# Score matmuls of two steps in one visit, one output chunk and one small product behind them, three score banks, and no loops, in an attention kernel on one core

## The chip, the cores and the metric

The kernel runs on one core of one Trainium2 chip. Its time is the device time of one execution in microseconds (us). PE is the matrix engine (TensorE), DVE is VectorE, ACT is ScalarE, POOL is GpSimd; SP is SyncE, which issues all transfers.

## The reference

Two layers on x of 8 batches x 512 positions x 128 channels: a selective-scan block, a top-1 mixture of 8 experts, a 16-head attention, and a graph of 6 attention nodes. What the change touches is the attention of the last two:

```
# _L1_attn_ref: 16 heads of 8 channels            # _mha, once per node: 8 heads of 16 channels
q = (x @ w_Q).reshape(Bs, Ts, H, HD)              qh = (q @ wq).reshape(B, S, H, dh)
scores = einsum('bhtd,bhsd->bhts', q, k)/sqrt(HD) scores = einsum('bqhd,bkhd->bhqk', qh, kh)/sqrt(dh)
probs = softmax(scores)                           attn = softmax(scores)
attn = einsum('bhts,bhsd->bhtd', probs, v)        return ctx @ wo
```

All softmaxes are over 512 keys.

## The kernel before

The work comes in three stages: the scan block (to about 390 us of the profile), the experts in the same stretch, and then the attention, which takes the rest. Only the attention is changed.

**Units.** The attention is a row of 64 units `u`. A unit is one batch with 8 heads. Units 0 to 15 are of the first kind (`kc`: the 16-head attention, two units per batch), units 16 to 63 of the node kind (`kn`: 6 nodes x 8 batches). The last eight also carry the final layer norms. A unit has two groups `k` of four heads; a group has eight steps `i`. `body(c, q, r)` of each engine writes one unit, with `u = 4 q + r`.

**A step.** The scores are computed twice. `scores` (L1049) makes a 128 x 512 tile of them in `bank_s`, of which DVE takes only the maxima (`reduce`, L1503). `scoresT` (L1072, two matmuls) makes the transposed scores, with the maximum already subtracted through extra rows of the operands, in one 1024-column slot of `bank_x`; ACT's `exp` (L838) reads the slot. A step issues, in this order on PE, one `scores`, the two `scoresT`, one `scores`. The score matmuls run 36 tiles ahead of the exponentials (`LEAD`). Both use 48 or 50 rows of one half of the array, `scores` the other half from `scoresT`, so that they run side by side:

```
for i in range(8):
    one, two = led(c, q, r, k, i)
    scores(*one)
    scoresT(x, k, i)
    scores(*two)
```

**Banks.** PSUM has eight banks: four are the two slots of `bank_x`, two are `bank_s`, one is `bank_o` (the output), one is `bank_m`. `scores` of tile N waits until the reduction of tile N - 2 is done (`need(pe, S["c_red"], N - 1)`).

**Between the steps.** `output` (L1089) multiplies the exponentials with the values: four heads in four 32-column parts of the array, in 4 calls of 512 columns per group (for the first kind 8 of 256). It stands after steps 0, 1, 4, 5 for nodes, after every step for the first kind. The small products are:
- `maxima` (L1059), the transpose of the maxima, into `bank_m`; ACT `ev_m` takes it out, SP puts it into the operands (`rows_m`);
- `turn` (L1103), four transposes of the output, into `bank_m`; DVE `divide` reads it in two instructions, a reciprocal (L1529) and a product (L1536);
- `out_proj` (L1123) into `bank_m`, read by DVE `node_out` (L1549);
- `value` (L1035), `turn_ctx` (L1113), `proj_q` (L1001), `proj_kh` (L1014), `proj_qh` (L1022), `turn_x3` (L1132), `turn_final` (L1143), each into the next slot of `bank_x`, in the ring with the exponentials, read by ACT.

**Order and loops.** Nothing schedules: each engine's order is written out in its `body`, and semaphores tie them. `units` (L277) runs units 0 to 3 straight, loops over q = 1, 2, runs q = 3, 4 straight, loops over q = 5 to 13 (units 20 to 55), and runs the last eight straight. A loop's turn is thus at units 24, 28, ... 52.

**DVE.** `parts` (L1514, L1517) prepares the maxima of a group at step 6; `divide` stands at step 4 for nodes, 6 for the first kind.

## Time and profile before

| | |
|---|---|
| median of 3 runs | 2368.41 us (2367.84 to 2372.26) |
| the profiled execution's own time | 2356.44 us |
| its span, first to last instruction | 2354.4 us |
| PE matmul busy | 2116.2 us, 90% |
| DVE busy | 1742.3 us, 74% |
| ACT busy | 1476.5 us, 63% |
| mean granted PE clock | 0.922 of 2.4 GHz |
| attention: first to last exponential | 420.9 to 2328.9 us |

A busy PE is not a PE at its peak: its records are as long as the passage through the array. What a piece costs is read from the distance between starts. Durations are from the one profiled execution, and sums are made against its span.

### The profile page before, as it was taken

How to read it: one execution, taken by the hardware profiler on the slowest of the kernel's cores; microseconds unless marked ns; L12 is line 12 of the kernel's file. 1: busy time of each engine (PE TensorE's matmuls, PEld its weight loads, DVE VectorE, ACT ScalarE, POOL GpSimd, SP SyncE). 2: the span in 40 equal slices, each digit the busy share in tenths (PEclk: the TensorE clock that was granted, in tenths of full speed). 3: DMA queues.
4: the chain of work that ended last, by engine and by line, in shares of the span. 5: the costliest groups of instructions: out<-in, count | busy, mean ns of one | idle time of the engine just before them, and what ended most of it. 6: DMA issues, size and time to landing. Idle time of an engine off the chain costs nothing.

```text
span 2354.4 us, 40695 instructions
## 1 busy us (share of the span) xinstructions
PE 2116.2 (90%) x11820; PEld 879.7 (37%) x11820; DVE 1742.3 (74%) x3501; ACT 1476.5 (63%) x2004; POOL 341.3 (14%) x385
## 2 busy tenths in 40 slices
PE   5758864999999999999999999999999999999995
PEld 2224431433434443343333334333333333333332
DVE  5847873677877777777677777677777677778884
ACT  4724540556656666777676767676767676776664
POOL 1101143000000011111011111010101111112223
PEclk9967885678998999999899999899999899999998
DMA  3010112322333345555465656555555555555521
GB/s 97 18 49 32 42 45 58 59 56 53 72 65 69 77 86 107 114 109 109 88 107 97 108 96 109 94 102 102 102 102 102 102 102 102 102 102 107 99 46 32
DMA packets 137173, 195.17 MB, mean 83 GB/s; under 512 B 20152, under 2 KB 55632, under 8 KB 137040
## 3 DMA queue, kind: packets, MB, share of 16 engines
q1 hardware_dynamic: 137040, 193.63, 42.6%
q8 instruction: 54, 0.88, 0.2%
q14 instruction: 79, 0.65, 0.1%
HBM read 75.45 MB, written 23.73 MB: 42 GB/s over the span
## 4 chain that ended last, share of the span: by engine, by line
PE 69%; DVE 15%; issue 8%; ACT 4%; POOL 2%; DMA 1%; DVEq 1%; SPq 0%; POOLq 0%; ACTq 0%
PE bank_s L1049 23%; PE bank_o L1089 19%; DVE big L1503 6%; PE bank_x L1072 5%; PE bank_m L1103 3%; PE bank_x L1035 3%; PE bank_x L1014 3%; ACT big L838 2%; PE bank_x L1001 2%; PE bank_m L1123 2%; PE bank_x L1022 2%; DVE big L1310 2%; PE bank_s L952 1%; DVE big L1301 1%; DVE big L1549 1%
## 5 line engine op out<-in xcount | busy, mean ns | idle before, releaser
L1503 DVE TENSOR_REDUCE big<-bank_s 128x1 f32<-128x512 f32 x2048 | 1338.2, 684 | 442.4 <-PE bank_s L1049 402.1
L838 ACT ACTIVATE big<-bank_x 128x1024 f32<-128x1024 f32 x1024 | 1046.1, 1022 | 477.8 <-PE bank_x L1072 469.5
L1049 PE MATMUL bank_s<-kst,qst 48*128 48x512 f32 x2048 | 864.4, 482 | 66.0 <-DVE big L1503 52.3
L1072 PE MATMUL bank_x<-qst,kst 50*128 50x512 f32 x2048 | 771.8, 458 | 5.1 <-ACT big L838 1.9
L1049 PEld LDWEIGHTS bank_s<-kst,qst 48*128 48x128 f32 x2048 | 365.4, 192 | 752.5 <-DVE big L1503 693.0
L1089 PE MATMUL bank_o<-big,at 128*32 128x512 f32 (+1 forms) x5104 | 598.6, 542 | 3.4 <-ACT big L838 2.0
L1072 PEld LDWEIGHTS bank_x<-qst,kst 50*128 50x128 f32 x2048 | 312.4, 191 | 29.2 <-ACT big L838 22.4
L618 POOL CAST at<-at 128x512 fp32r<-128x512 f32 x112 | 68.2, 609 | 1375.9 <-ACT at L769 1086.8
L1089 PEld LDWEIGHTS bank_o<-big,at 128*32 128x32 f32 x5104 | 103.5, 110 | 182.1 <-issue 164.1
L620 POOL TENSOR_TENSOR at<-at 128x512 fp32r<-128x512 f32 x112 | 143.1, 1277 | 10.1 <-POOL at L618 0.3
L806 ACT ACTIVATE at<-bank_o 128x512 f32<-128x512 f32 x128 | 76.3, 596 | 66.6 <-PE bank_o L1089 66.6
L1310 DVE TENSOR_SCALAR big<-big 128x128 f32<-128x128 f32 x192 | 62.4, 397 | 41.7 <-POOL big L611 40.7
L1103 PE MATMUL bank_m<-ident,at 128*128 128x128 f32 x512 | 87.3, 295 | 1.0 <-ACT at L806 0.7
L846 ACT ACTIVATE big<-bank_x,big 128x128 f32<-128x128 f32 x256 | 68.7, 376 | 26.2 <-DVE big L1449 14.6
L609 POOL TENSOR_TENSOR big<-big,eps_ln 128x4 f32<-128x4 f32 x40 | 13.7, 344 | 470.5 <-DVE big L1305 470.5
L1149 PE MATMUL bank_x<-xw,big 128*128 128x512 f32 x128 | 77.5, 751 | 0.0
L1103 PEld LDWEIGHTS bank_m<-ident,at 128*128 128x128 f32 x512 | 55.6, 144 | 51.6 <-issue 49.3
L1493 DVE TENSOR_REDUCE big<-big 128x128 f32<-128x1024 f32 x32 | 60.9, 1904 | 5.9 <-ACT big L846 5.9
L1035 PE MATMUL bank_x<-at 128*128 128x128 f32 x384 | 60.4, 304 | 0.0
L1035 PEld LDWEIGHTS bank_x<-at 128*128 128x128 f32 x384 | 50.8, 206 | 19.8 <-issue 19.8
L1022 PE MATMUL bank_x<-at 128*128 128x512 f32 x96 | 53.9, 643 | 3.2
L1123 PE MATMUL bank_m<-big,at 128*128 128x512 f32 x96 | 54.9, 655 | 0.7 <-issue 0.7
(151 smaller groups left out, 1499.0 us busy)
## 6 DMA issues: line engine op xcount, KB each, us to landing
at<-nodes_d SPq DMA_DIRECT2D x144, 256.0 KB, 5.2
kst<-at SPq DMA_DIRECT2D x288, 128.0 KB
qst<-at SPq DMA_DIRECT2D x288, 128.0 KB
nodes_d<-big SPq DMA_DIRECT2D x48, 256.0 KB, 2.9
at<-w_d SPq DMA_DIRECT2D x48, 193.0 KB, 5.3
at<-x2T_d SPq DMA_DIRECT2D x32, 256.0 KB, 3.8
kst<-at SPq DMA_DIRECT2D x128, 64.0 KB
qst<-at SPq DMA_DIRECT2D x128, 64.0 KB
```

The source lines that it names most:

```text
L620: pool.tensor_tensor(dst[:, 1, :], src, dst[:, 0, :], ALU.subtract).then_inc(done, n)
L838: act.activation(PT[:, kp, h, :, :], ring.take()[0].rearrange("p (c n) -> p c n", c=2), ACT.Exp, scale=x.c.scale).then_inc(S["c_ex"], 1)
L1022: pe.matmul(to[:, 0:L], st_qk[x.half][:, P:2 * P], q_sb[x.r], start=True, stop=True).then_inc(S["c_qh_ps"], 1)
L1035: mm = pe.matmul(to[:, k * n:(k + 1) * n], t[:, P + k * P:P + (k + 1) * P], w, start=True, stop=True)
L1049: pe.matmul(bank_s[:, n % 2, :], qst[rows, x.r, h, t * P:(t + 1) * P], kst[rows, x.r, h, :], start=True, stop=True).then_inc(S["c_s_ps"], 1)
L1072: mm = pe.matmul(sec(to, j), kst[rows, x.r, h, kc_ * P:(kc_ + 1) * P], qst[rows, x.r, h, :], start=True, stop=True)
L1089: mm = pe.matmul(bank_o[COL * h:COL * (h + 1), cols], vaug[x.half][:, 2 * kp + j, GH * k + h, :], PT[:, kp, h, j, cols], start=(kp == 0 an ...
L1103: mm = pe.transpose(bank_m[:, t * P:(t + 1) * P], ot_sb[:, t * P:(t + 1) * P], ident[:, :])
L1123: pe.matmul(bank_m[:, :], st_o[x.half][:, 0:P], ctxT, start=True, stop=True).then_inc(S["c_wo_ps"], 1)
L1149: mm = pe.matmul(sec(bank_x[:, t % 2, :], j), hT[:, t * P:(t + 1) * P], xw[:, j * 512:(j + 1) * 512], start=True, stop=True)
L1310: i = dve.tensor_scalar(dst[:, t * D:(t + 1) * D], src[:, t * D:(t + 1) * D], mv_[:, t, 0:1], rs_[:, t:t + 1], ALU.subtract, ALU.mult)
L1503: dve.tensor_reduce(nm[:, k, at_n:at_n + 1], bank_s[:, n % 2, :], AX.X, ALU.max, negate=True).then_inc(S["c_red"], 1)
```

## The change

1. **No loops.** `units` writes all 64 units out on every engine. The functions that chose slots for a loop's turn are gone.
2. **Two steps per visit.** On PE the four score matmuls and the four transposed ones of steps 2v and 2v + 1 stand together. Behind each such visit stands one `output` of 512 columns x 4 heads (both kinds of unit), and then one small product, in (k = 1, v = 2) two.
3. **Three score banks.** `bank_m` joins `bank_s`; tiles go round the three. `scores` of tile N waits for the reduction of tile N - 3; `maxima` takes a turn in the round.
4. **Small products in the exponentials' slots.** All others, `turn` and `out_proj` now too, take the second half (columns 512 to 1023) of the next slot of `bank_x`. A `scoresT` waits for each half separately.
5. **DVE.** `divide` stands at step 6 for all; `node_out` before the reductions of step 2 of group 1 (it stood behind step 0); the final norm is spread otherwise. On POOL `split` goes ahead of `final_sum`.

The arithmetic is the same. The diff, cut to this:

```diff
         def units(e, body):
-            for r in range(RING):
-                body(kc, 0, r)
-            with e.Fori(1, QC - 1) as it:
...
+            for q in range(QU):
                 for r in range(RING):
                     body(None, q, r)
...
+        ring_place = {item: n for n, item in enumerate(ring_order())}
+        ring_slot = lambda kind, n: bank_x[:, ring_place[kind, n] % 2, :]
+        ring_half = lambda kind, n: bank_x[:, ring_place[kind, n] % 2, L:2 * L]
+        def score_bank(place):
+            return (bank_s[:, 0, :], bank_s[:, 1, :], bank_m[:, :])[place % 3]
...
             def scores(x, k, n):
-                need(pe, S["c_red"], N - 1)
+                to = score_slot(score_place(N), S["c_red"], N + 1)
...
             def scoresT(x, k, i):
-                to = slot(S["c_ex"], 8 * G + i + 1)
+                s_ = ring[0] % 2
                 for j in range(2):
+                    if ring_readers[s_][j] is not None:
+                        need(pe, *ring_readers[s_][j])
+                    ring_readers[s_][j] = (S["c_ex"], 8 * G + i + 1)
...
+                for k in range(2):
+                    done = (last, 1) if k == 0 else (x, 0)
+                    for v in range(4):
+                        for i in (2 * v, 2 * v + 1):
+                            one, two = led(c, q, r, k, i)
+                            scores(*one)
+                            scoresT(x, k, i)
+                            scores(*two)
+                        if v == 0:
+                            maxima(*led_group(c, q, r, k))
+                        if v < 2:
+                            output(*done, 1, v)
+                        else:
+                            output(x, k, 0, v - 2)
+                        if (k, v) == (0, 1):
+                            value(at_(c, q, r + 1))
+                        if v == 2:
+                            turn(*done)
+                        if (k, v) == (0, 3):
+                            turn_ctx(last)
+                        if (k, v) == (1, 0):
+                            out_proj(last)
+                        if (k, v) == (1, 1):
+                            proj_q(ahead)
+                        if (k, v) == (1, 2):
+                            proj_kh(ahead)
+                        if (k, v) == (1, 3):
+                            proj_qh(ahead)
...
             def body(c, q, r):            # DVE
+                        if (k, i) == (1, 2):
+                            node_out(last)
                         for j, group in enumerate(led(c, q, r, k, i)):
-                            if i == paced(x, 4, 6):
-                                divide(*((last, 1) if k == 0 else (x, 0)), j)
+                            if i == 6:
+                                divide(*done, j)
                             reduce(*group)
                             if i == 6:
                                 parts(*read_group(c, q, r, k), j)
```

In the listings of order that follow, `c_red` is a finished reduction, `c_ex` an exponential, `c_ot_ev` a finished `divide`, `c_kf_ev`, `c_q_ev` ACT's evictions of `proj_kh`, `proj_q`; the first word of a row is the line in its own kernel.

PE, node unit, group 1, the steps 2 and 3. Before (L1001 is `proj_q`, L1103 `turn`):

```order
L1049 MATMUL bank_s<-kst,qst 128x512 [waits c_red]
L1072 MATMUL bank_x<-qst,kst 128x512 [waits c_ex]
L1072 MATMUL bank_x<-qst,kst 128x512
L1049 MATMUL bank_s<-kst,qst 128x512 [waits c_red]
L1103 MATMUL bank_m<-ident,at 128x128 [waits c_mT_ev,c_pv_ev]
L1103 MATMUL bank_m<-ident,at 128x128 x3
L1049 MATMUL bank_s<-kst,qst 128x512 [waits c_red]
L1072 MATMUL bank_x<-qst,kst 128x512 [waits c_q_ev]
L1072 MATMUL bank_x<-qst,kst 128x512
L1049 MATMUL bank_s<-kst,qst 128x512 [waits c_red]
L1089 MATMUL bank_o<-big,at 32x512 [waits c_v_ev,c_pv_ev,c_ex]
L1089 MATMUL bank_o<-big,at 32x512 x3
```

and now (L1076 is `scores`, L1104 `scoresT`, L1119 `output`, L1028 `proj_q`):

```order
L1119 MATMUL bank_o<-big,at 32x512 x4
L1028 MATMUL bank_x<-at 128x512 [waits c_ex,c_qk1]
L1076 MATMUL bank_s<-kst,qst 128x512 [waits c_red]
L1104 MATMUL bank_x<-qst,kst 128x512 [waits c_ex] x2
L1076 MATMUL bank_m<-kst,qst 128x512 [waits c_red]
L1076 MATMUL bank_s<-kst,qst 128x512 [waits c_red]
L1104 MATMUL bank_x<-qst,kst 128x512 [waits c_ex]
L1104 MATMUL bank_x<-qst,kst 128x512 [waits c_q_ev]
L1076 MATMUL bank_s<-kst,qst 128x512 [waits c_red]
L1119 MATMUL bank_o<-big,at 32x512 [waits c_v_ev,c_pv_ev,c_ex]
```

Two steps stand together, four `scores` each waiting for its reduction; one `output` and one small product are behind them.

PE, the end of the same group, steps 6 and 7 (before: L1014 `proj_kh`, L1022 `proj_qh`; the output behind steps 4 and 5 stands ahead of these rows):

```order
L1049 MATMUL bank_s<-kst,qst 128x512 [waits c_red,c_stk1]
L1072 MATMUL bank_x<-qst,kst 128x512 [waits c_ex]
L1072 MATMUL bank_x<-qst,kst 128x512
L1049 MATMUL bank_s<-kst,qst 128x512 [waits c_red]
L1014 MATMUL bank_x<-at 128x512 [waits c_ex,c_qk0]
L1049 MATMUL bank_s<-kst,qst 128x512 [waits c_red]
L1072 MATMUL bank_x<-qst,kst 128x512 [waits c_ex]
L1072 MATMUL bank_x<-qst,kst 128x512
L1049 MATMUL bank_s<-kst,qst 128x512 [waits c_red]
L1022 MATMUL bank_x<-at 128x512 [waits c_kf_ev,c_q_ev]
```

and now, from `turn` (L1132) and `proj_kh` (L1041) behind steps 4 and 5:

```order
L1132 MATMUL bank_x<-ident,at 128x128 [waits c_ex,c_pv_ev]
L1132 MATMUL bank_x<-ident,at 128x128 x3
L1041 MATMUL bank_x<-at 128x512 [waits c_ex,c_qk1]
L1076 MATMUL bank_m<-kst,qst 128x512 [waits c_red,c_stk2]
L1104 MATMUL bank_x<-qst,kst 128x512 [waits c_ex]
L1104 MATMUL bank_x<-qst,kst 128x512 [waits c_ot_ev]
L1076 MATMUL bank_s<-kst,qst 128x512 [waits c_red] x2
L1104 MATMUL bank_x<-qst,kst 128x512 [waits c_ex]
L1104 MATMUL bank_x<-qst,kst 128x512 [waits c_kf_ev]
L1076 MATMUL bank_m<-kst,qst 128x512 [waits c_red]
L1119 MATMUL bank_o<-big,at 32x512 x4
```

`turn` was two steps further up and in its own bank; now it is in a ring slot, and the second `scoresT` of step 6, right behind the first `scores`, waits for `c_ot_ev`.

DVE, node unit, from `divide` to `parts`. Before:

```order
L1529 RECIPROCAL big<-bank_m 128x16 [waits c_ot_ps]
L1503 TENSOR_REDUCE big<-bank_s 128x1 [waits c_s_ps]
L1536 TENSOR_TENSOR big<-bank_m,big 128x4x64 [waits c_sum]
L1503 TENSOR_REDUCE big<-bank_s 128x1 [waits c_s_ps] x4
L1514 CAST big<-big 128x2x8 [waits c_mT_ps,c_red]
L1503 TENSOR_REDUCE big<-bank_s 128x1 [waits c_s_ps]
L1517 TENSOR_TENSOR big<-big 128x2x8 [waits c_link]
```

and now:

```order
L1539 RECIPROCAL big<-bank_x 128x16 [waits c_ot_ps]
L1514 TENSOR_REDUCE big<-bank_s 128x1 [waits c_s_ps]
L1525 CAST big<-big 128x2x8 [waits c_mT_ps,c_red]
L1546 TENSOR_TENSOR big<-bank_x,big 128x4x64 [waits c_sum]
L1514 TENSOR_REDUCE big<-bank_s 128x1 [waits c_s_ps]
L1528 TENSOR_TENSOR big<-big 128x2x8 [waits c_link]
```

The product that ends `divide` (L1536, now L1546) keeps one reduction ahead of it, but that is now the first reduction of a visit, and a cast (L1525) stands between.

## Rows read from the trace of the kernel before

**Rows 1.** The page: busy time of each engine, the chain by engine.

```profile
PE 2116.2 (90%) x11820; PEld 879.7 (37%) x11820; DVE 1742.3 (74%) x3501; ACT 1476.5 (63%) x2004; POOL 341.3 (14%) x385
...
PE 69%; DVE 15%; issue 8%; ACT 4%; POOL 2%; DMA 1%; DVEq 1%; SPq 0%; POOLq 0%; ACTq 0%
```

**Rows 2.** Windows: busy us of PE, PEld, DVE, ACT, POOL; clock, DMA, GB/s. Node units.

```profile
911.80:1026.70 114.90, 112.34 (x634) 44.71 (x633) 91.06 (x177) 82.87 (x101) 16.06 (x18) 0.99 0.56 107
1026.70:1139.00 112.30, 110.77 (x636) 44.66 (x632) 88.87 (x164) 82.78 (x100) 14.81 (x17) 1.00 0.59 108
1139.00:2092.00 953.00, 915.90 (x5060) 366.58 (x5056) 715.10 (x1313) 663.15 (x801) 118.94 (x129) 0.97 0.56 101
1139.00:1261.10 122.10, 116.99 (x636) 46.47 (x632) 89.52 (x164) 82.94 (x101) 14.90 (x17) 0.94 0.55 98
1261.10:1378.10 117.00, 112.86 (x636) 45.76 (x632) 89.27 (x164) 82.84 (x100) 14.82 (x17) 0.99 0.57 102
```

**Rows 3.** Timeline at a loop's turn: start, length, engine, operation, [idle before <-what ended it].

```profile
1141.05 0.50 PE L1049 MATMUL bank_s<-kst,qst 48*128 48x512 f32 x1 [1.18 <-DVE big L1503]
...
1144.27 0.79 PE L1049 MATMUL bank_s<-kst,qst 48*128 48x512 f32 x1 [2.41 <-DVE big L1503]
```

**Rows 4.** Timeline, node unit: two steps, the maxima and an output between.

```profile
1084.30 0.28 PE L1059 MATMUL bank_m<-ident,big 128*32 128x128 f32 x1
...
1084.51 1.07 PE L1089 MATMUL bank_o<-big,at 128*32 128x512 f32 x8
...
1085.51 0.49 PE L1049 MATMUL bank_s<-kst,qst 48*128 48x512 f32 x1
...
1085.51 0.49 PE L1072 MATMUL bank_x<-qst,kst 50*128 50x512 f32 x1
...
1085.84 0.39 PE L1049 MATMUL bank_s<-kst,qst 48*128 48x512 f32 x1
...
1086.04 1.29 DVE L1503 TENSOR_REDUCE big<-bank_s 128x1 f32<-128x512 f32 x2 [0.58 <-PE bank_s L1049]
...
1086.17 1.16 PE L1035 MATMUL bank_x<-at 128*128 128x128 f32 x8
...
1087.26 0.50 PE L1049 MATMUL bank_s<-kst,qst 48*128 48x512 f32 x1
```

**Rows 5.** Timeline, same unit: turn and out_proj, each with the step behind it.

```profile
1088.02 0.66 PE L1103 MATMUL bank_m<-ident,at 128*128 128x128 f32 x4
...
1088.60 0.50 PE L1049 MATMUL bank_s<-kst,qst 48*128 48x512 f32 x1
...
1089.14 0.50 PE L1049 MATMUL bank_s<-kst,qst 48*128 48x512 f32 x1
...
1089.57 1.06 PE L1089 MATMUL bank_o<-big,at 128*32 128x512 f32 x8
...
1094.74 1.12 PE L1123 MATMUL bank_m<-big,at 128*128 128x512 f32 x2
...
1095.80 0.49 PE L1049 MATMUL bank_s<-kst,qst 48*128 48x512 f32 x1
```

**Rows 6.** Timeline, same unit: VectorE's order and the PE matmul that waits for it.

```profile
1092.77 0.69 DVE L1503 TENSOR_REDUCE big<-bank_s 128x1 f32<-128x512 f32 x1 [0.39 <-PE bank_s L1049]
...
1093.38 0.16 DVE L1514 CAST big<-big 128x16 fp32r<-128x16 f32 x1
...
1093.52 0.49 PE L1049 MATMUL bank_s<-kst,qst 48*128 48x512 f32 x1
```

**Rows 7.** Groups by line and form, 700 to 2200 us.

```profile
L1536 DVE TENSOR_TENSOR big<-bank_m,big 128x256 f32<-128x256 f32 x86 | 35.6, 414 | 0.0
L1549 DVE SCALAR_TENSOR_TENSOR big<-bank_m,at 128x512 f32<-128x512 f32 x43 | 31.9, 741 | 0.0
```

**Rows 8.** Windows: four units of the first kind; 14 us of another such unit.

```profile
548.30:669.60 121.30, 113.20 (x860) 48.97 (x862) 94.00 (x187) 75.24 (x90) 9.97 (x12) 0.96 0.33 69
...
751.00:765.00 14.00, 13.37 (x69) 5.40 (x69) 8.22 (x16) 5.86 (x7) 0.00 (x0) 0.52 0.22 37
```

More of the change, by code:

```diff
@@ L813, in ev_cT @@
                 need(act, S["c_wo_ps"], x.un)
-                act.activation(ctxT, ring.take()[0][:, 0:L], ACT.Copy).then_inc(S["c_cT_ev"], 1)
+                act.activation(ctxT, ring_half("cT", x.u), ACT.Copy).then_inc(S["c_cT_ev"], 1)
             def ev_x3T(x):
@@ L829, in ev_final @@
                 need(act, S["f_nm"], j)
-                act.activation(nT, ring.take()[0][:, 0:L], ACT.Copy).then_inc(S["f_tT_ev"], 1)
+                act.activation(nT, ring_half("f", x.u), ACT.Copy).then_inc(S["f_tT_ev"], 1)
             def exp(x, k, i):
@@ L1020, in proj_qh @@
                 need(pe, S["c_q_ev"], x.un + 1)
-                to = slot(S["c_qf_ev"], x.un + 1)
-                pe.matmul(to[:, 0:L], st_qk[x.half][:, P:2 * P], q_sb[x.r], start=True, stop=True).then_inc(S["c_qh_ps"], 1)
+                to = slot("qh", x.u, S["c_qf_ev"], x.un + 1)
+                pe.matmul(to, st_qk[x.half][:, P:2 * P], q_sb[x.r], start=True, stop=True).then_inc(S["c_qh_ps"], 1)
             def value(x, to=None):
@@ L1088, in output @@
                 for h in range(GH):
-                    mm = pe.matmul(bank_o[COL * h:COL * (h + 1), cols], vaug[x.half][:, 2 * kp + j, GH * k + h, :],
-                                   PT[:, kp, h, j, cols], start=(kp == 0 and step == 0),
-                                   stop=(kp == 1 and step == steps - 1))
-                if step == steps - 1:
+                    mm = pe.matmul(bank_o[COL * h:COL * (h + 1), :], vaug[x.half][:, 2 * kp + j, GH * k + h, :],
+                                   PT[:, kp, h, j, :], start=(kp == 0 and j == 0), stop=(kp == 1 and j == 1))
+                if j == 1:
                     mm.then_inc(S["c_pv_ps"], 1)
@@ L1121, in out_proj @@
                 need(pe, S["c_cT_ev"], x.un + 1)
-                misc(S["c_wo_ev"], x.un + 1)
-                pe.matmul(bank_m[:, :], st_o[x.half][:, 0:P], ctxT, start=True, stop=True).then_inc(S["c_wo_ps"], 1)
+                to = slot("wo", x.u, S["c_wo_ev"], x.un + 1)
+                pe.matmul(to, st_o[x.half][:, 0:P], ctxT, start=True, stop=True).then_inc(S["c_wo_ps"], 1)
             def turn_x3(x):
@@ L1278, in _ @@
             units(pe, body)
             end = at_(kn, QU - 1, RING - 1)
-            for step in range(2):
-                output(end, 1, 1, step, 2)
+            for j in range(2):
+                output(end, 1, 1, j)
             turn(end, 1)
```

245 lines of the change are left out of this document (114 added, 131 removed).

## The prediction

> **What bounds the kernel now.** The page comes first: PE is busy 90% of the span, DVE 74%, ACT 63%, and PE makes up 69% of the chain of waits [rows 1]. An average over stages says little, so the windows come next. Four node units fill 112.3 us, 28.08 us each; in them PE is busy for 110.8 us and DVE for 88.9, 22.2 us per unit [rows 2]. A node unit is thus at PE's pace, with 6 us of slack on DVE. The next 32 node units do the same work per unit and take 953.0 us, where eight times 112.3 would be 898.4: 54.6 us more, at eight turns of the loop. The timeline shows a turn: PE sits idle for 1.18 us and again for 2.41 us, and behind that a matmul takes 0.79 us instead of 0.50 [rows 3], a lower clock (the two windows with a turn show 0.94 and 0.99 in place of 1.00, and lose 9.8 and 4.7 us [rows 2]).
>
> Last, the timeline of a node unit at full clock. A PE record is longer than its cost, so I take distances between starts. `scores` and `scoresT` start together at 1085.51, the second pair at 1085.84, the next kind of product at 1086.17: a step costs 0.66 us, 0.33 per pair. An output costs 1085.51 - 1084.51 = 1.00, the maxima 0.21, `value` 1.09 [rows 4]; `turn` 0.58, a product of 512 columns (`out_proj`, and by it the three `proj`) 1.06 [rows 5]; `turn_ctx`, four transposes like `turn`, I take at 0.58 too. A unit's 16 steps (10.6), 8 outputs (8.0), 2 maxima (0.4), 2 turns (1.2) and the rest (1.09 + 0.58 + 4 x 1.06 = 5.9) add up to 26.1; the 2.0 us missing to 28.08 are short waits.
>
> **The change, part by part.**
>
> *Loops.* The eight turns go: -54.6 us, and about -1 for the one turn inside the first kind's loop. Straight code could cost gaps for the loading of instructions. Units 16 to 19 are straight already and take 114.9 us with the change of kind among them and one short drop of the clock, against 112.3 for the loop's first pass [rows 2]. I take nothing; 2.6 us per four units, 35 us in all, would be the upper bound.
>
> *Two steps per visit: what it saves.* The 0.33 us of a pair is more than its streaming. An output is two passes and takes 1.00 with its switch [rows 4], so some 0.43 per pass of four parallel matmuls, each in two halves; I estimate 0.22 us for a pair that follows pairs. A visit of four pairs would be 0.33 + 0.22 + 0.22 + 0.33 = 1.10 against 1.32 in two visits. With 8 visits this saves 1.8 us per unit, if nothing waits. The Trainium skill says it too (TensorEngine Tiling (Array Packing), Key Properties): changing the tiling mode drains the TensorE. By that rule alone the change would be a gain everywhere, and that is a rival below.
>
> *What it costs: the fourth score matmul.* With three banks, tile N + 3 waits for the reduction of N, and both are in one visit. From the start of the first `scores` to its reduction 0.53 us (1085.51 to 1086.04 [rows 4]); the reduction 0.69; its release 0.06 (1092.77 + 0.69 to 1093.52 [rows 6]). So the fourth `scores` starts 1.27 us into the visit, not 0.77. From a lone `scores` to an output 0.43 (1089.14 to 1089.57 [rows 5]). A visit with its output is then 1.27 + 0.43 + 1.00 = 2.70 us, where two steps and an output now cost 0.66 + 0.66 + 1.00 = 2.32. The saving turns into a loss, in each of 8 visits: 21.6 us. DVE does not push this further: four reductions start 0.61 apart (1092.77 to the cast at 1093.38 [rows 6]) and are done 3.1 us into a visit of 2.7 to 4 us, and the next visit's first `scores` waits only for the second of them.
>
> *The small products* cost as before, 5.9 + 2 x 0.58 = 7.1. The maxima now wait for the reduction of the visit's second tile: 0.53 + 0.61 + 0.69 + 0.06 = 1.89, and 0.21 more; the output starts at 2.10 and not at 1.70, +0.4 twice: 0.8.
>
> *`turn` in the ring.* Its slot comes free with the product that ends `divide`. DVE reaches that behind the first reduction of the visit of steps 6 and 7 and a cast: 0.53 + 0.61 + 0.08 + 0.41 for the product [rows 7] + 0.06 = 1.69. In group 0 it is the last `scoresT` of the visit that waits (1.69 instead of 1.27: +0.42). In group 1 `proj_kh` takes a slot too, so that the waiting one is the second `scoresT` of step 6; behind it stand three pairs: 1.69 + 0.33 + 0.22 + 0.33 = 2.57 against 1.70, +0.87.
>
> *`node_out`* (0.74 [rows 7]) now stands ahead of the reductions of the visit behind `out_proj`. The product lands 0.06 into that visit (1094.74 + 1.12 = 1095.86, the step starts 1095.80 [rows 5]), so the first reduction starts at 0.77, not 0.53: +0.24. It was between reductions before and cost PE next to nothing.
>
> A node unit: 21.6 + 7.1 + 0.8 + 0.4 + 0.9 + 0.2 = 31.0 us, 2.9 more than 28.1. ACT is no limit (20.7 us busy per unit [rows 2]), and eviction of a small product (0.6) ends before its half is wanted at 0.77 of the next visit. Of the 48 node units I count 45 (the first follows another kind, the last has nothing ahead): +130.5 us.
>
> *First kind.* Its output goes from 16 halves to 8 wholes, and there are 16 switches less each way. By the same sum a unit is 21.6 + 0.8 + 1.3 + 1.09 + 1.16 + 1.06 = 27.0, without the layer norm. Four units take 121.3 now [rows 8], 30.3 each with the norms of every second and a little low clock. I take -5 us for all 16; bounds -25 to +25.
>
> *Clock.* The turns' low clock is in the 54.6. But the 1.2 GHz level also comes in first-kind units, 14 us at 0.52 of full speed after DVE's norm holds up the score matmuls [rows 8], and the new waits for `divide` stop PE for about 1.4 us in every node unit, near the idle time that preceded the low clock at the loop's turn [rows 3]. A price: a turn, wait and clock together, costs 4.7 to 9.8. I take +10 us (two to four drops); between nothing and one in every second unit, 100 us.
>
> Sum: 2354.4 - 54.6 - 1 + 130.5 - 5 + 10 + 2.0 (what lies around the span) = **2436 us**. The profiled execution is 12 us under the median of the runs (2356.4 to 2368.4); I leave that out, since part of it may go with the loops.
>
> **The rivals.**
>
> *The clock falls often* (chance 0.15). For it: the two waits per unit, in a stage that is less dense than before. Against it: in the 112.3 us window short waits of up to half a microsecond change nothing. Twenty drops more at 4 to 5 us: 2436 + 90 = 2526 us. The Trainium skill (TensorE: Matmul & The Clock Gate, Part 1) says that activity releases the throttle and idleness brings it back; the trace agrees at the loop's turns.
>
> *The mode drains decide, the waits do not* (0.07, faster). This is the skill's rule on mode switches carried through: the third bank takes the wait off the fourth `scores`, or reductions start so early that 1.27 is 0.8. Then a node unit is 8 x (1.10 + 1.00) + 7.1 + 0.4 = 24.3 at PE's limit; DVE's 22.2 busy and the waits for `divide` leave about 26. -2.1 x 45 with the loops: 2354.4 - 55.6 - 94.5 + 2 = 2206 us. Against it: DVE takes a tile every 0.61 us and cannot have finished N at 0.8 when it starts at 0.53. It decides the sign below 29.3 us per node unit: there 45 x 1.2 eats the 55 us of the loops.
>
> *The loops' gain and the visits' loss cancel* (0.06). If the `divide` wait in group 1 and the maxima's wait are hidden and pairs are cheaper, a unit is 29.3: 2356 us, within 0.2% or a little to either side.
>
> *It is dearer than I say, at full clock* (0.07): if the weights of the third and fourth pair are not hidden (0.33 per pair throughout), the pairs behind the fourth wait cost the same, but group 1's last visit and the ring waits grow: 31.5 to 32, 2460 to 2480 us.
>
> **How the numbers follow.** The forecast, 0.65, is a unit of 30.2 to 31.6 and few drops: 2395 to 2480. The range 2385 to 2510 takes in the dearer case and the nearer half of the clock case and leaves out the two cheap cases. A measurement of this kernel tells about 0.2% (5 us) from no change. Faster by more: 0.07 + 0.03 of the cancelling case = 0.10; within: 0.03; slower: 0.87.
>
> **What would show it.** The windows of four node units: 124 us each and all alike, with no jump at every fourth unit. In the timeline a fourth `scores` 1.27 us behind the first, released by DVE; in the group-1 visit behind `proj_kh` a `scoresT` at 1.7 us, released by the product of `divide`; DVE still at 22 us busy per unit and idle for 8 to 9. Wrong if node units are under 29.3 us, if the fourth `scores` starts before 1.1, or if the clock is at its low level in more than a few windows.

## The result

| | median | runs | ratio to before, 95% interval |
|---|---|---|---|
| before | 2368.12 us | 4 (2357.5 to 2372.26) | |
| changed | 2442.73 us | 4 (2435.92 to 2443.85) | 1.0316 [1.0277, 1.0355] |

Slower by 3.2%. The prediction was 2436 us in a range of 2385 to 2510, with 0.87 on slower. The changed kernel's profiled execution has a span of 2434.1 us (before: 2354.4) and a mean granted clock of 0.937 (before: 0.922). The changed kernel is slower although its clock is higher.

The page of the changed kernel, busy time and chain, answers to [rows 1]:

```profile
PE 2072.7 (85%) x10812; PEld 858.9 (35%) x10812; DVE 1731.5 (71%) x3501; ACT 1447.6 (59%) x2004; POOL 343.7 (14%) x385
...
PE 61%; DVE 24%; issue 8%; POOL 3%; SPq 1%; DMA 1%; ACT 1%; DVEq 0%; POOLq 0%; ACTq 0%
```

DVE does no more work than before, and yet its share of the chain of waits has gone from 15% to 24%: PE now waits for DVE. The costliest groups say where. The last field is the engine's idle time ahead of the group and what ended most of it:

```profile
L1104 PE MATMUL bank_x<-qst,kst 50*128 50x512 f32 x2048 | 687.0, 442 | 131.8 <-DVE big L1546 131.1
L1076 PE MATMUL bank_s<-kst,qst 48*128 48x512 f32 x1365 | 571.2, 460 | 37.0 <-DVE big L1514 17.1
```

The first is `scoresT`, waiting for the product of `divide` (L1546): 131 us in all, where the kernel before has 5.1 us of idle time ahead of its `scoresT`. The second is `scores`. Its wait for the third bank shows as little idle time of PE, because the last `scoresT` of the visit is still streaming for most of it, and yet it delays everything behind it.

The windows of four node units answer to [rows 2]: here two of the changed kernel. (Columns as in [rows 2]: busy us of PE, PEld, DVE, ACT, POOL, which is GpSimd; clock, DMA share, GB/s.)

```profile
1090.60:1216.80 126.20, 114.83 (x634) 45.20 (x631) 89.35 (x165) 80.75 (x100) 14.91 (x16) 0.99 0.50 95
1217.00:1343.40 126.40, 115.02 (x635) 45.62 (x633) 89.57 (x165) 80.89 (x101) 15.06 (x17) 0.99 0.49 94
```

Four units take 126.3 us where 112.3 stood [rows 2]. DVE's busy time is unchanged (89.4 against 88.9), as the clock nearly is.

For the whole run I cut each trace at the start of the first exponential of a unit (each unit has 16). All later comparisons use this table, in us:

| | before | changed | difference |
|---|---|---|---|
| up to unit 0 | 420.8 | 412.9 | -7.9 |
| first kind, units 0 to 15 | 490.9 | 455.4 | -35.5 |
| node units 16 to 55 | 1180.2 | 1264.4 | +84.2 |
| last eight units | 236.9 | 270.9 | +34.0 |
| behind the last exponential | 25.5 | 30.5 | +5.0 |
| span | 2354.4 | 2434.1 | +79.7 |

The 7.9 us ahead of unit 0 were not looked into; the loops are not their cause, for with the loops written out (experiment 1) unit 0 starts at 421.2 us.

Of the changed kernel's node units to 55 most take 31.2 us, and every third or fourth (ten of them) takes 32.8. The timeline shows why. First a visit with an output, at full clock (start, length, engine, operation, [idle before and what ended it]):

```profile
1186.43 0.49 PE L1076 MATMUL bank_m<-kst,qst 48*128 48x512 f32 x1
...
1186.77 0.39 PE L1076 MATMUL bank_s<-kst,qst 48*128 48x512 f32 x1
...
1187.00 0.40 PE L1076 MATMUL bank_s<-kst,qst 48*128 48x512 f32 x1
...
1187.71 0.49 PE L1076 MATMUL bank_m<-kst,qst 48*128 48x512 f32 x1
1188.13 1.06 PE L1119 MATMUL bank_o<-big,at 128*32 128x512 f32 x8
1189.13 1.16 PE L1062 MATMUL bank_x<-at 128*128 128x128 f32 x8
```

The fourth `scores` starts 1.28 us behind the first, its output 0.42 later, and the next product 1.00 after that: 2.70 us. The second pair starts 0.34 behind the first, the third 0.23 behind the second. Now the visit of steps 6 and 7 in group 0 and in group 1:

```profile
1193.51 0.50 PE L1076 MATMUL bank_s<-kst,qst 48*128 48x512 f32 x1
...
1195.19 0.50 PE L1104 MATMUL bank_x<-qst,kst 50*128 50x512 f32 x1 [0.72 <-DVE big L1546]
```

```profile
1209.56 0.50 PE L1076 MATMUL bank_s<-kst,qst 48*128 48x512 f32 x1
...
1210.10 0.69 DVE L1514 TENSOR_REDUCE big<-bank_s 128x1 f32<-128x512 f32 x1 [1.03 <-PE bank_s L1076]
1210.51 0.61 POOL L637 CAST at<-at 128x512 fp32r<-128x512 f32 x1 [24.41 <-ACT at L786]
1210.71 0.44 DVE L1525 CAST big<-big 128x16 fp32r<-128x16 f32 x1
1211.07 0.41 DVE L1546 TENSOR_TENSOR big<-bank_x,big 128x256 f32<-128x256 f32 x1
...
1211.53 0.50 PE L1104 MATMUL bank_x<-qst,kst 50*128 50x512 f32 x1 [1.47 <-DVE big L1546]
...
1212.42 1.71 PE L1119 MATMUL bank_o<-big,at 128*32 128x512 f32 x8
```

The waiting `scoresT` starts 1.68 us into its visit in group 0 and 1.97 in group 1, and in group 1 PE is idle for 1.47 us. The output behind it takes 1.71 us instead of 1.06: the clock is at 1.2 GHz there. A window on that stretch gives its level (0.50 of 2.4 GHz) and its length:

```profile
1212.70:1216.10 3.40, 3.40 (x12) 0.53 (x4) 1.37 (x4) 1.30 (x2) 0.00 (x0) 0.50 0.61 120
```

Note the row between: DVE's cast takes 0.44 us, with GpSimd's cast of a weight block at its side. In group 0, with GpSimd idle, the same cast takes 0.16. Experiments 10 and 11 rest on this.

### The profile page after: what moved, and what is told of

It is laid out like the page before. It is cut to its first block, busy times and chain, and to the rows that moved or that the text cites. A ratio compares the mean times of both kernels' runs of the same rounds, so it can differ in the third digit from the quotient of the medians.

```text
span 2434.1 us, 32371 instructions
## 1 busy us (share of the span) xinstructions
PE 2072.7 (85%) x10812; PEld 858.9 (35%) x10812; DVE 1731.5 (71%) x3501; ACT 1447.6 (59%) x2004; POOL 343.7 (14%) x385
## 4 chain that ended last, share of the span: by engine, by line
PE 61%; DVE 24%; issue 8%; POOL 3%; SPq 1%; DMA 1%; ACT 1%; DVEq 0%; POOLq 0%; ACTq 0%
PE bank_o L1119 20%; DVE big L1514 13%; PE bank_s L1076 10%; PE bank_x L1104 5%; PE bank_m L1076 5%; PE bank_x L1132 3%; PE bank_x L1062 3%; PE bank_x L1049 3%; PE bank_x L1041 2%; PE bank_x L1152 2%; PE bank_x L1028 2%; DVE big L1546 2%; DVE big L1321 2%; DVE big L1525 1%; DVE big L1559 1%
## 5 line engine op out<-in xcount | busy, mean ns | idle before, releaser
L1514 DVE TENSOR_REDUCE big<-bank_s 128x1 f32<-128x512 f32 x1365 | 896.3, 682 | 289.6 <-PE bank_s L1076 273.0
L1104 PE MATMUL bank_x<-qst,kst 50*128 50x512 f32 x2048 | 687.0, 442 | 131.8 <-DVE big L1546 131.1
L1076 PE MATMUL bank_s<-kst,qst 48*128 48x512 f32 x1365 | 571.2, 460 | 37.0 <-DVE big L1514 17.1
L1514 DVE TENSOR_REDUCE big<-bank_m 128x1 f32<-128x512 f32 x683 | 465.9, 682 | 140.4 <-PE bank_m L1076 140.0
L1119 PE MATMUL bank_o<-big,at 128*32 128x512 f32 x4096 | 560.5, 620 | 0.0
L1104 PEld LDWEIGHTS bank_x<-qst,kst 50*128 50x128 f32 x2048 | 344.6, 189 | 272.8 <-DVE big L1546 178.6
L1076 PEld LDWEIGHTS bank_s<-kst,qst 48*128 48x128 f32 x1365 | 245.8, 190 | 332.0 <-DVE big L1514 240.1
L1076 PE MATMUL bank_m<-kst,qst 48*128 48x512 f32 x683 | 314.8, 461 | 15.7 <-DVE big L1514 9.4
L1076 PEld LDWEIGHTS bank_m<-kst,qst 48*128 48x128 f32 x683 | 129.6, 190 | 165.3 <-DVE big L1514 124.0
L1119 PEld LDWEIGHTS bank_o<-big,at 128*32 128x32 f32 x4096 | 81.2, 108 | 121.2 <-issue 103.8
L1132 PEld LDWEIGHTS bank_x<-ident,at 128*128 128x128 f32 x512 | 53.5, 140 | 108.1 <-issue 106.5
L1132 PE MATMUL bank_x<-ident,at 128*128 128x128 f32 x512 | 83.9, 287 | 0.7 <-ACT at L823 0.7
```

The source lines that it names most:

```text
L1076: pe.matmul(to, qst[rows, x.r, h, t * P:(t + 1) * P], kst[rows, x.r, h, :], start=True, stop=True).then_inc(S["c_s_ps"], 1)
L1104: mm = pe.matmul(sec(bank_x[:, s_, :], j), kst[rows, x.r, h, kc_ * P:(kc_ + 1) * P], qst[rows, x.r, h, :], start=True, stop=True)
L1119: mm = pe.matmul(bank_o[COL * h:COL * (h + 1), :], vaug[x.half][:, 2 * kp + j, GH * k + h, :], PT[:, kp, h, j, :], start=(kp == 0 and j == ...
L1132: mm = pe.transpose(to[:, t * P:(t + 1) * P], ot_sb[:, t * P:(t + 1) * P], ident[:, :])
L1514: dve.tensor_reduce(nm[:, k, at_n:at_n + 1], score_bank(score_place(16 * (2 * x.u + k) + n)), AX.X, ALU.max, negate=True).then_inc(S["c_re ...
```

## The experiments

**1. The loops alone.** The kernel before, with its loops written out.

```
-            with e.Fori(1, QC - 1) as it:
-                for r in range(RING):
-                    body(kc, it, r)
...
+            for q in range(QU):
+                for r in range(RING):
+                    body(None, q, r)
```

> The kernel before with its loops written out, nothing else changed. Theory (the eight loop turns cost 54.6 us in wait and low clock, the rest of the change is a loss): node units at 28.1 us all through, no window with a jump at every fourth unit, 2368 - 56 = 2312 us. Rival (straight code loads its instructions as dearly as a loop turns): about 2368 us, with gaps of 2 to 3 us spread over the units.

Measured: 2296.31 us against 2373.88, ratio 0.9703 [0.9621, 0.9786]. Units 16 to 55 take 1125.7 us, 54.5 less than before, and from unit 18 on each takes 28.1. The window that holds four of them, where one turn stood at 122.1 and 117.0 us in [rows 2]:

```profile
1122.30:1234.70 112.40, 110.84 (x636) 44.62 (x634) 89.17 (x165) 82.84 (x100) 14.86 (x17) 1.00 0.59 107
```

The term of the loops was right to the tenth, and straight code shows no gap of its own. The first kind took 474.6 us, 16 less than before. Repeated on another chip (experiment 8) it took 481.9, so 7 of those 16 us are within what the clock does there from run to run. The first kind is also why the run is 16 us under the 2312 expected.

**2. The divide's place.** The changed kernel, with both instructions of `divide` ahead of the first reduction of its visit.

```
-                            if i == 6:
-                                divide(*done, j)
+                            if (i, j) == (6, 0):
+                                divide(*done, 0)
+                                divide(*done, 1)
                             reduce(*group)
```

> The changed kernel, with both instructions of divide ahead of the first reduction of step 6 instead of around it. Theory (scoresT waits for the slot that turn holds until divide is done, 1.69 us in group 0 and 1.97 in group 1): group 0's last scoresT starts at 1.5 (the first reduction starts later, at 0.8), group 1's wait is gone (fourth scores at 1.28). Node unit 31.2 to about 30.0 us, and the low clock at every third or fourth unit gone: 2443 - 55 to - 75, that is 2370 to 2390 us. Rival (the fourth scores alone sets the pace, and the ring waits hide behind it): within 10 us of 2443.

Measured: 2352.35 us, ratio to before 0.9909 [0.9878, 0.9941]. A unit takes 29.8 us, the 32.8-us ones are gone, and between 770 and 2121 us the clock never leaves its full level. Units 16 to 55 fall from 1264.4 to 1192.8 us. One place in DVE's queue turns a kernel 3.2% slower than before into one 0.9% faster. The fourth `scores` of the two visits starts 1.47 and 1.29 us into them, as expected. The waits for `divide` were worth 1.4 us in a unit at full clock (the sum had 0.42 and 0.87 for them), and with the low clock behind them 1.8 (71.6 us over 40 units); the run is 18 us below the 2370 to 2390 expected. GpSimd still gets in DVE's way in group 1: the cast takes up to 0.44 us there, and the small product behind the next reduction 0.85 instead of 0.16. But `divide` now stands ahead of both, so PE's `scoresT` does not wait for them.

**3. The output between the two steps of a visit.** The changed kernel, with the output moved to behind the first step.

```
+                            if i == 2 * v and v < 2:
+                                output(*done, 1, v)
+                            elif i == 2 * v:
+                                output(x, k, 0, v - 2)
```

> The changed kernel, with the output put between the two steps of a visit instead of behind them: one step per visit again, three banks and the ring as they are. Theory (the fourth scores' wait of 0.5 us comes from four score matmuls in one visit): that wait is gone, the third and fourth scores start without waiting for a reduction; but the exponentials then start later, and the first scoresT of the next visit waits for its slot, about 0.6 us behind the short products: node unit about 30.5 us, 2415 us. Rival 1 (mode switches decide): eight more switches each way make it 31.2 + 8 x 0.33 = 33.8 us, 2560 us. Rival 2 (only the fourth scores and nothing new): 28.2 us, 2310 us.

Measured: 2492.5 us, ratio 1.0482 [1.038, 1.0584]. At full clock a unit is 30.8 us, little less than 31.2 and near the 30.5 of the theory. The third bank's wait now hides behind the output, and the timeline shows what comes in its place. `scoresT` waits for ACT's exponential, 0.60 us behind the `scores` that it used to start with:

```profile
1252.62 0.49 PE L1076 MATMUL bank_s<-kst,qst 48*128 48x512 f32 x1
1253.22 0.50 PE L1104 MATMUL bank_x<-qst,kst 50*128 50x512 f32 x1
```

Each pair costs 0.33 again, and group 1's wait for `divide` is as long as it was (1.97 us, PE idle for 1.47). How the rest divides among the three was not settled. The run is 77.5 us above the 2415 expected. Most of that is the first kind, which takes 511.8 us instead of 455.4, with twelve stretches at the lower clock; their cause stays open. Two windows of it, four node units and the first kind:

```profile
1243.70:1366.80 123.10, 112.23 (x636) 42.63 (x637) 91.34 (x165) 81.06 (x100) 15.05 (x17) 1.00 0.51 98
417.60:929.40 511.80, 448.36 (x2393) 176.24 (x2396) 363.94 (x730) 299.26 (x365) 42.44 (x51) 0.90 0.32 68
```

So the place of the output is no way out of the third bank's wait.

**4. A shorter reduction.** The changed kernel, with each reduction over the first 256 of its 512 keys. Maxima of half the keys are not the maxima, and the exponentials' scale is cut to 0.02 of its value so that none overflows; the output is another one.

```
-score_bank(score_place(16 * (2 * x.u + k) + n)), AX.X
+score_bank(score_place(16 * (2 * x.u + k) + n))[:, 0:256], AX.X
```

> The changed kernel, with each reduction over the first 256 of the 512 keys only, and the exponentials' scale cut to 2% so that nothing overflows; its output is not the reference's. Theory (a reduction stands in the path of the fourth scores, of the maxima and of divide): a reduction of 0.35 us starts the fourth scores at 0.53 + 0.35 + 0.06 = 0.94 instead of 1.28, node unit 27.3 to 28 us, 2443 - 160 = 2280 us. Rival (PE's own work sets the pace): node unit stays above 30.5 us.

Measured: 2227.2 us, ratio 0.9391 [0.9304, 0.9478]; a unit 28.3 us, a little above the 27.3 to 28 expected. The run is 53 us below the 2280 expected; the first kind alone takes 409.8 us, 45.6 less than in the changed kernel. The timeline:

```profile
1006.28 0.50 PE L1076 MATMUL bank_s<-kst,qst 48*128 48x512 f32 x1
...
1006.82 0.42 DVE L1514 TENSOR_REDUCE big<-bank_s 128x1 f32<-128x256 f32 x1 [2.06 <-PE bank_s L1076]
...
1007.30 0.49 PE L1076 MATMUL bank_s<-kst,qst 48*128 48x512 f32 x1
1007.49 0.76 DVE L1514 TENSOR_REDUCE big<-bank_s 128x1 f32<-128x256 f32 x2
1007.72 1.07 PE L1119 MATMUL bank_o<-big,at 128*32 128x512 f32 x8
```

The fourth `scores` now comes at 1.02 us = 0.54 + 0.42 + 0.06, and the output at 1.44, 0.26 earlier, as the reduction is 0.26 shorter. This is the chain that the prediction gave the third bank: first matmul, its reduction, its release. Eight visits by 0.26 are 2.1 of the 2.9 us that the unit lost. The maxima, which wait for two reductions, save 0.26 more in each of their two visits, and group 1's wait for `divide` goes from 1.97 to 1.43 us, 0.28 more than a visit's 0.26.

**5. Whole outputs in the first kind.** Experiment 1's kernel, with the first kind's output in 512 columns.

```
-                steps = paced(x, 2, 4)
+                steps = 2
```

> This is the kernel before with its loops written out (2296.3 us), with one more edit: the first kind's output, which it makes in four products of 256 columns, is made in two of 512 as the changed kernel does. What of the first kind's shortening (490.9 us before, 474.6 without loops, 455.4 in the changed kernel, from its first to its last exponential) comes from whole output products? Theory A, the switches between kinds of products: each quarter product and each pair after it pays about 0.1 us for the change of tile form, so 16 units of 16 switches fewer pay, of which a part lies beside other work: the first kind takes 455 to 465 us, the run 2277 to 2287 us. Theory B, the shortening came from the layer's normalising being placed otherwise and from fewer low-clock stretches: whole products here only make the scores late (a 512-column product holds TensorE 1.0 us where the window between two pairs is shorter), so the first kind takes 475 to 485 us, and the run 2296 to 2306 us.

Measured: 2330.15 us, ratio 0.9804 [0.9717, 0.9892]; the first kind 511.8 us. Worse than theory B had it: a unit without a norm takes 27.9 to 28.2 us at full clock where experiment 1 has 26.9, and the clock is at its lower level in 19 stretches of the first kind. Theory A falls, and the run is 24 us above even theory B's range. In the timeline of one such unit `scores` waits for reductions again and again (0.54 and 0.18 us behind one output). Whole outputs do not explain why the changed kernel's first kind is shorter.

**6. The last layer norm's place.** Experiment 2's kernel, with the norm's four steps one to two visits later.

```
-                        if (k, i) == (1, 7):
-                            final_norm(last, 0)
...
+                        if (k, i) == (0, 0):
+                            final_norm(older, 0)
```

> This is the changed kernel with both divide instructions ahead of the reduction (2352.4 us), with one more edit: the four steps of the last layer norm come one to two visits later, in the unit after, so that VectorE no longer waits for the transposed output of a unit just made while reductions are queued behind that wait. In the last eight units (266.4 us there, three of them at 37.5 to 39.4 us) each theory differs. Theory A, the waits of these steps on VectorE stop the reductions and TensorE's clock falls after the stop: the long units shrink to 32 to 34 us, and the run to 2325 to 2340 us. Theory B, it is the work of these steps itself (about 2 to 3 us on VectorE in a unit), wherever it stands: the long units stay at 35 us or more and the run at 2345 to 2357 us.

Measured: 2320.72 us, ratio 0.9747 [0.9662, 0.9832]; the last eight units 232.5 us instead of 266.4, the long ones 31.4 us, and no low clock in them. Theory A, by a little more than it claimed. What it removed is seen in the changed kernel at the first of these units:

```profile
2197.15 0.87 DVE L1312 BATCH_NORM_STATS2 big<-big 128x6 f32<-128x128 f32 x4 [1.64 <-ACT big L847]
...
2198.48 0.66 DVE L1514 TENSOR_REDUCE big<-bank_m 128x1 f32<-128x512 f32 x1
...
2199.19 0.79 PE L1076 MATMUL bank_m<-kst,qst 48*128 48x512 f32 x1 [1.53 <-DVE big L1514]
```

The statistics stand in DVE's queue for a tile that ACT has only just taken out (L847), two reductions wait behind them, PE waits for the reductions, and its next matmuls take 0.79 us. Three units of this stretch in the changed kernel and with the norm's steps moved:

```profile
2197.20:2310.80 113.60, 97.24 (x489) 41.17 (x487) 82.68 (x196) 62.89 (x79) 29.89 (x34) 0.89 0.43 80
```

```profile
2119.90:2214.30 94.40, 89.28 (x491) 36.85 (x487) 82.01 (x196) 62.19 (x79) 30.12 (x34) 1.00 0.54 96
```

The same work on DVE (82.7 and 82.0 us) in 113.6 and in 94.4 us.

**7. The first kind's norm, dealt out.** Experiment 1's kernel; the four instructions of `normalise` go behind four reductions, one each.

```
+                            if k == 1 and 2 <= i < 4:
+                                residual(last, 2 * (i - 2) + j + 2)
...
-                            residual(last, 2)
```

> This is the kernel before with its loops written out (2296.3 us), with one more edit: the first kind's normalising, four instructions in a row on VectorE ahead of the reductions of one step (2.1 us together), is dealt out one instruction behind each of four reductions. Theory A, the block stops the reductions and with them scores and exponentials, and the clock falls behind it: its units, 30 to 34 us in that kernel, go to about 29 us, the first kind from 474.6 to 450 to 465 us and the run to 2272 to 2287 us. Theory B, VectorE has no slack in these units, so the 2.1 us are paid wherever they stand: the first kind stays at 470 us or more and the run at 2290 to 2300 us.

Measured: 2278.4 us, ratio 0.9565 [0.9485, 0.9646], but the profiled execution was the longest of the four. The medians speak for A, the profile for neither, so it was run again beside experiment 1's kernel.

**8 and 9. Both again on one chip.**

> The kernel before with its loops written out, once more and on the same chip as the next one. Its first kind differs from execution to execution by the stretches at a lower clock that it draws, so its time is 2285 to 2312 us as before, and its second kind's full units are at 28.1 us to the tenth again. A first kind of 470 to 480 us is expected by both theories of the next kernel.

> The same with the first kind's normalising dealt out behind four reductions. In the one profile taken so far its units of the first kind at full clock were 29.5 to 29.9 us against 30.3, and yet the first kind took 488.7 us, since two stretches of 30.7 us and one of 23.9 us at the lower clock lay in it. Theory A, the block on VectorE costs about 0.8 us in each of 7 units and leads to some of the low-clock stretches: the median is 8 to 25 us below that of the kernel beside it. Theory B, the gain is the 5 us of the units alone, and the rest was the draw of the clock: the medians differ by less than 8 us.

Measured: 2294.18 us, 0.9693 [0.9648, 0.9738], and 2277.08 us, 0.9623 [0.9585, 0.9661]. The difference of 17 us is theory A's, and the first kind takes 481.9 and 464.6 us. One profile says little here: experiment 7's, of the same kernel as experiment 9, has a first kind of 488.7 us with 96 us of it at the lower clock, where experiment 9's has 10.

The block's length needs another look. In the traces it takes 2.0 us in one unit and 1.1 in another, so its length is not its own. The kernel before, at the place of [rows 8]:

```profile
748.86 2.11 DVE L1310 TENSOR_SCALAR big<-big 128x128 f32<-128x128 f32 x4
```

```profile
748.84 1.28 POOL L620 TENSOR_TENSOR at<-at 128x512 fp32r<-128x512 f32 x1
```

Of the four, the first takes 1.34 us and the others 0.34. It ends with GpSimd's product. In six of that kernel's units the first instruction starts within GpSimd's product and takes 1.24 to 1.34 us; in the seventh it does not and takes 0.34. In the changed kernel all take 0.34:

```profile
487.56 1.10 DVE L1321 TENSOR_SCALAR big<-big 128x128 f32<-128x128 f32 x4
```

The Trainium skill has it (SBUF — State Buffer, Who interferes with whom): VectorE and GpSimd share one pair of ports, copies, casts and `tensor_scalar` can take it, and who comes second is blocked until the other's instruction has ended. The traces agree: up to 1.0 us lost per product, 0.28 per cast.

Dealing the norm out did not take this encounter away. In experiment 9 the last of the four instructions still meets GpSimd's product (500.65 to 501.26 its cast, 501.41 to 502.68 its product) and takes 0.90 us:

```profile
500.93 0.41 DVE L1558 TENSOR_SCALAR big<-big 128x128 f32<-128x128 f32 x1
501.26 0.68 DVE L1492 TENSOR_REDUCE big<-bank_s 128x1 f32<-128x512 f32 x1
501.86 0.90 DVE L1558 TENSOR_SCALAR big<-big 128x128 f32<-128x128 f32 x1
```

The four together take as long as the block did (2.0 us), and the even units are 29.5 us at full clock for 30.3. So part of the loss comes from the 2 us standing in a row ahead of the reductions, whatever made them long.

**10. The norm whole, one step earlier.**

```
+                        if (k, i) == (1, 2):
+                            residual(last, 2)
                         if (k, i) == (1, 3):
-                            residual(last, 2)
```

> The kernel before with its loops written out, with the first kind's normalising whole, as there, but placed one step (two reductions) earlier on VectorE. In the traces so far its first instruction takes 1.24 to 1.34 us where GpSimd's 1.28-us product of a weight block runs beside it (six of seven units of the kernel before), and 0.34 us where none runs (all units of the changed kernel); the four take 2.0 to 2.1 us or 1.10. One step earlier it falls into time in which VectorE is idle (1.35 us behind PE) and GpSimd too. Theory A, the two engines get in each other's way, and that delay, not the length of the block, holds up the scores and brings the lower clock: the four instructions take 1.1 us, the first kind's even units 29 to 29.6 us at full clock, the first kind 450 to 465 us and the run 2262 to 2280 us. Theory B, it is the block in a row that stops the reductions: 29.8 us or more, and the run at 2283 us or above.

Measured: 2272.35 us against 2362.91, ratio 0.9619 [0.9579, 0.9658]. Theory A, again by a little more: the block takes 1.11 us, the even units 28.5 us at full clock (30.3 in experiment 1, 29.5 in experiment 9), the first kind 456.7, with 7 us at the lower clock (34 and 51 in experiments 1 and 8). Two things changed at once, though: the block no longer meets GpSimd, and it stands where DVE had idle time. No run of the old form holds the one fixed and moves the other. GpSimd's product, in the second row, starts when the block is long done.

```profile
500.80 1.11 DVE L1299 TENSOR_SCALAR big<-big 128x128 f32<-128x128 f32 x4
```

```profile
503.32 1.27 POOL L609 TENSOR_TENSOR at<-at 128x512 fp32r<-128x512 f32 x1
```

**11. The divide's product ahead of the cast.** The changed kernel, with the first reduction left where it is.

```
                             reduce(*group)
+                            if (i, j) == (6, 0):
+                                divide(*done, 1)
```

> The changed kernel (2442.7 us), with one edit: behind the first reduction of the visit of steps 6 and 7, the product of the divide comes ahead of the cast of the maxima and not behind it. In group 1 of every second-kind unit that cast takes 0.44 us instead of 0.16 and overlaps GpSimd's cast of a weight block for 0.41 us, and a scoresT waits for the product behind it: 1.97 us into its visit where group 0's is 1.69. Theory A, the two engines' overlap is what makes group 1's wait long, and the long wait what brings the 3.4-us stretch of low clock in every third or fourth unit: the product is done 0.35 us earlier in group 1 and 0.08 in group 0, the units take 30.7 to 30.8 us and the stretches are gone: 48 units by 0.45 and 13 by 1.6, 2395 to 2425 us. Theory B, the product is delayed by GpSimd as the cast was, or another wait ends the same visit: the units stay at 31.1 to 31.2 us and the run within 8 us of the changed kernel.

Measured: 2398.23 us, ratio to before 1.016 [1.0117, 1.0203], 44.5 us under the changed kernel's median on another chip (by the two ratios to before, 37 us). Node units take 30.8 us, and from unit 16 to unit 55 (864 to 2095 us) the clock stays at its full level. Theory A. Group 1's visit (its first `scores` starts at 1227.31):

```profile
1228.45 0.41 DVE L1546 TENSOR_TENSOR big<-bank_x,big 128x256 f32<-128x256 f32 x1
1228.78 0.17 DVE L1525 CAST big<-big 128x16 fp32r<-128x16 f32 x1
1228.92 0.50 PE L1104 MATMUL bank_x<-qst,kst 50*128 50x512 f32 x1 [1.11 <-DVE big L1546]
```

The wait ends at 1.61 us instead of 1.97, and the product, which reads PSUM, takes its 0.41 us beside GpSimd's cast (1228.26 to 1228.87) as it does without one. DVE's cast meets only the last 0.09 us of GpSimd's and takes 0.17.

## Why the prediction was right

**The visit** (21.6 us of a unit): 1.27 + 0.43 + 1.00 was predicted and 1.28 + 0.42 + 1.00 measured. The pair that follows a pair was estimated at 0.22 from the output's passes and is 0.23. Experiment 4 shows the chain: shorten the reduction and the visit shortens by as much.

**The waits for `divide`.** Group 0: 1.69 predicted, 1.68 measured. Group 1: 1.69 predicted, 1.97 measured. The step that failed put DVE's cast at 0.08 us of its time; GpSimd's cast makes it 0.36 (1210.71 to 1211.07). The output behind it stands at 2.86 (1212.42 - 1209.56), not 2.57. That is 0.3 us per unit, and the unit came to 31.2 us at full clock for the 31.0 of the sum.

The small terms can be read from the same trace (the unit from 1216.1 to 1247.3 us). The two visits with maxima have their output at 2.17 us, not 2.10: 0.1 for both together. `node_out` delays its visit's fourth `scores` to 1.51 us, +0.24 as predicted. `turn` and `proj_kh` one behind the other take 1.45 us and not 1.64, which gives 0.2 back. With these the eight visits add up to 31.2.

**The loops.** -54.6 predicted, -54.5 measured (experiment 1). The node units of 16 to 55 went from 1125.7 us without loops to 1264.4: 40 by 3.1 us, and 16 us for ten units with a low clock.

**The clock.** +10 us in two to four drops was predicted. In the node units to 55 it is about 16 us, in ten drops of 3.4 us that cost 1.6 us each; an eleventh lies in unit 16. The last eight units have seven more stretches, of 3.4 to 10.2 us, where the kernel before has one. The number thus lies between the forecast's two to four and the twenty of the rival in which the clock falls often. That rival's price was wrong, for it took a loop's turn, 4 to 5 us, and much of that is the turn's own wait (PE idle for 1.18 and 2.41 us [rows 3]). Experiment 11 has no drop in the node units to 55; what its edit changed there is that PE's idle time in group 1 is 1.11 us for 1.47.

By two of its own signs the prediction was wrong here. It wanted four node units at 124 us and all alike; they take 126.3, and every third or fourth unit is longer. And it named as a sign of being wrong that the clock is at its low level in more than a few windows. What it had wrong is the step from PE's idle time behind `divide` to the clock: the wait was seen, and two to four drops were put to it where every third or fourth unit has one.

**The first kind** is the worst term: -5 was predicted, between -25 and +25, and -35.5 measured. Its form costs about what was said: without loops and without the collision on DVE (experiment 10) the old form takes 456.7 us, the changed one 455.4. What the sum lacked is that collision. It took the norm and the low clock behind it [rows 8] as a cost that would stay. About 1 of the block's 2.1 us was an encounter with GpSimd, which a shift of DVE against GpSimd can make or remove, and in the changed kernel it is gone. Taking it away together with the block's place (experiment 10 against 1 and 8) saves 18 to 25 us of the first kind, and by the runs' ratios to before 18 to 20 us of the whole. That the loop's turn and the draw of the clock make up the rest is argued: the stretches at the lower clock add up to 68 us in the first kind before and to 10 in the changed kernel. The encounter does not explain them all, for experiment 3 has none of it and 82 us at the lower clock.

**The last eight units.** Six of them were counted like other node units, 17 us; +34.0 measured. The sum left out that the norm's statistics now stand where a wait for them stops the reductions and so PE. Experiment 6 puts their place at fault, not their work.

**The sum.** It gave a span of 2434.3 us, and 2434.1 was measured. That closeness is luck. Against the sum the first kind came out 29.5 us shorter (-35.5 for -6); the last eight units 16.6 longer; the clock in the node units 6 longer; the full-clock time of units 16 to 55 9.6 longer (122.7 us for 39 by 2.9); and the two ends 2.9 shorter. The sign and the main term are no luck.

**The rivals.** That the mode drains decide falls with the fourth `scores` at 1.28 us: the visit saved its switches (a pair 0.23 instead of 0.33) and lost more to the bank. Experiment 4 shows the other side of it, a unit of 28.3 us once the reduction is short. That loops and visits cancel falls with 31.2 us per unit, though experiment 2 reaches it by moving DVE's instructions alone.

**What beats both kernels.** The kernel before without loops (2296 us) and with the norm one step earlier (2272 us, 3.8% faster than before). The changed form at its best here (experiment 6) takes 2321 us. So the changed form as a whole loses 1.7 us per node unit even with `divide` in its better place (29.8 against 28.1). Merged visits, the third bank and the small products in the ring were not tried apart.

## What to carry to other kernels

When steps are merged to save switches, work out the chain of each buffer that is now used twice in a visit: first write, its reader, the release. If the reader takes longer than the merged writes, the saving turns into a wait. Before a duration from a trace is taken as the cost of an instruction, look at its shortest instance and at what GpSimd did beside the long ones: the long one may be an encounter that the change will move. It costs time only where something waits behind it, as experiments 2 and 11 show. And a queue of DVE whose head waits for a tile just made stops every reduction behind it: in the last eight units the same instructions, one to two visits later, cost 34 us less (266.4 to 232.5).

## What the runs showed of the hardware

- VectorE's `TENSOR_SCALAR` from and to SBUF (128 x 128, f32) takes 0.34 us alone and up to 1.34 beside GpSimd's 1.28-us product; its cast of 128 x 16 takes 0.16 us alone, 0.44 beside GpSimd's 0.61-us cast; a `TENSOR_TENSOR` of 128 x 16 within SBUF takes 0.16 us alone and 0.85 beside GpSimd's product (experiment 2). A product that reads one operand from PSUM takes 0.41 us in both cases, and the reductions from PSUM stay at 0.67 to 0.69.
- A stretch at 1.2 GHz can be as short as 3.4 us and still recur all through a dense stage: in ten of forty units, at the same place each time, 2.6 to 3.1 us after a 1.47-us idle time of PE began, and each costing 1.6 us; of the other thirty units twenty-nine had the same idle time and no such stretch behind it. Experiment 3, with the same idle time, has eight units with stretches of 3.4 to 10.2 us among its forty. Where PE's longest idle time was 1.1 us (experiment 11), 1.0 (experiment 4) or 0.5 (experiment 2), none appeared in forty units. No run gives a limit, though: an eleventh stretch of the changed kernel, in unit 16, came behind 0.45 and 0.54 us.
- A loop's turn over four units costs 4.7 to 9.8 us on this kernel; the same code written out costs none of it.
- Fewer and larger output products made the first kind slower: with whole outputs alone it was 30 to 37 us longer than with halves (511.8 against 474.6 and 481.9), with units of 27.9 to 28.2 us at full clock for 26.9 and 102 us at the lower clock for 34 and 51.
